# Routing to experts by pairs of positions: 128x128 transposes, a block-diagonal router, groups of 8 positions, ranks over 32, 24 and 7 positions

## What is computed

```
logits = xf @ Wr + br                       # 8064 rows x 64 experts
topk_logits, topk_idx = top_k(logits, 2)
gates = softmax(topk_logits)
for e in range(64):
    y = relu(xf @ W1[e] + b1[e]) @ W2[e] + b2[e]
    out = out + combine[:, e:e + 1] * y     # combine holds the gates of the two chosen
```

## Time and profile before

| | |
|---|---|
| median of 3 runs | 884.67 us (881.72 to 885.47) |
| the profiled execution: its own time | 888.75 us |
| the profiled execution: span, first to last instruction | 886.8 us |
| DVE busy | 645.4 us (73%) |
| POOL busy | 551.6 us (62%) |
| PE busy | 501.2 us (57%) |
| ACT busy | 339.2 us (38%) |
| granted clock of TensorE, mean | 0.741 |

### The profile page before, as it was taken

One profiled execution on the slowest core, in us unless ns is written; L12 is line 12 of the kernel. 1 busy time (PEld: TensorE's weight loads), 2 busy tenths in 40 slices (PEclk: granted clock), 3 DMA queues, 4 the chain that ended last, 5 costly groups with the idle time before them and its releaser, 6 DMA issues.

```text
span 886.8 us, 8725 instructions
## 1 busy us (share of the span) xinstructions
PE 501.2 (57%) x2132; PEld 320.0 (36%) x2132; DVE 645.4 (73%) x1160; ACT 339.2 (38%) x597; POOL 551.6 (62%) x398
## 2 busy tenths in 40 slices
PE   4916903365666665575556920002999999980340
PEld 3815801121211121121116910001777777760240
DVE  1379548999999989999974999991444444459951
ACT  2311384555555455454527710000444444430110
POOL 1002204699999999999940007777777167757774
PEclk9965655677787787878785555555999999995565
DMA  6999900000000000000000000302899899961131
GB/s 229 366 136 108 30 0 0 0 0 0 1 0 0 0 0 0 0 0 0 0 0 1 1 0 27 89 25 62 229 262 265 230 256 263 269 192 26 25 99 37
DMA packets 100734, 71.63 MB, mean 81 GB/s; under 512 B 29330, under 2 KB 87314, under 8 KB 100690
## 3 DMA queue, kind: packets, MB, share of 16 engines
q1 hardware_dynamic: 73154, 54.39, 28.0%
q0 software_dynamic: 8064, 8.27, 3.5%
q10 hardware_dynamic: 19472, 8.47, 3.3%
HBM read 48.12 MB, written 29.29 MB: 87 GB/s over the span
## 4 chain that ended last, share of the span: by engine, by line
POOL 35%; PE 22%; DVE 15%; issue 15%; SPq 4%; DMA 4%; ACT 3%; POOLq 1%; DVEq 0%; ACTq 0%
POOL hh_ring L419 13%; PE ps L611 8%; POOL w_ring L404 8%; POOL sorted_rows L438 7%; POOL xt L446 7%; PE ps L600 4%; DMA x_w<-packed 3%; PE ps L470 3%; SPq L328 2%; PE ps L538 2%; DVE mi L1072 1%; PE ps L521 1%; PE ps L593 1%; DVE hh_ring L1004 1%; DVE w_ring L1060 1%
## 5 line engine op out<-in xcount | busy, mean ns | idle before, releaser
L538 PE MATMUL ps<-hh_ring,ident 128*128 128x512 f32 x272 | 181.7, 807 | 153.1 <-POOL hh_ring L419 116.4
L438 POOL DMA_INDIRECT sorted_rows<-xp,slot_i x126 | 122.1, 969 | 115.0 <-DVE slot_i L1098 76.9
L404 POOL TENSOR_TENSOR w_ring<-xt,bc 128x1024 f32<-128x1024 f32 x64 | 153.8, 2405 | 37.3 <-DVE xt L973 37.3
L446 POOL DMA_INDIRECT xt<-expert_out,slot_i x126 | 120.7, 958 | 65.6 <-issue 37.8
L419 POOL TENSOR_TENSOR hh_ring<-hh_ring,bc 128x1024 f32<-128x1024 f32 x63 | 148.4, 2356 | 17.9 <-DVE hh_ring L1004 14.6
L538 PEld LDWEIGHTS ps<-hh_ring,ident 128*128 128x128 f32 x272 | 58.2, 234 | 275.8 <-POOL hh_ring L419 184.7
L1004 DVE TENSOR_TENSOR_SCAN hh_ring<-ps,w_ring 128x1024 f32<-128x1024 f32 x64 | 145.9, 2280 | 0.1
L611 PE MATMUL ps<-x_w 128*128 128x192 f32 x504 | 117.0, 355 | 0.0
L744 ACT ACTIVATE ps<-dt_t,a_exp 128x1024 f32<-128x1024 f32 x64 | 71.5, 1118 | 79.9 <-DVE w_ring L982 79.9
L748 ACT ACTIVATE ps<-dt_t,a_exp 128x1024 f32<-128x1024 f32 x64 | 71.5, 1118 | 65.1 <-DVE hh_ring L1004 65.1
L1172 DVE COPY x_w<-ps 128x128 f32<-128x128 f32 x126 | 36.8, 292 | 72.0 <-PE ps L611 69.0
(11 more groups left out here) (174 smaller groups left out, 707.9 us busy)
## 6 DMA issues: line engine op xcount, KB each, us to landing
x_w<-packed SPq DMA_DIRECT2D x252, 96.5 KB
sorted_rows<-pad_rows SPq DMA_DIRECT2D x2, 4096.0 KB, 18.0
x_w<-sorted_rows SPq DMA_DIRECT2D x32, 256.0 KB
expert_out<-x_w ACTq DMA_DIRECT2D x126, 64.0 KB
packed<-in_L_ffn_W SPq DMA_DIRECT2D x3, 2048.0 KB, 36.2
x_w<-in_x SPq DMA_DIRECT2D x7, 448.0 KB, 10.1
sorted_rows<-xp,slot_i POOLq DMA_INDIRECT x126, 2.1
xt<-expert_out,slot_i POOLq DMA_INDIRECT x126, 2.4
```

The costliest lines, as they stand in the source:

```text
L404: pool.tensor_tensor(w_ring[:, k % 4, :].rearrange("p (d s) -> p d s", s=S), up3[:, bass.ds(c * DC, DC), :], bc[:, k:k + 1, :].broadcast_t ...
L438: pool.indirect_dma_start(out=sorted_rows[k], out_offset=bass.IndirectOffsetOnAxis(ap=slot_i[:, k, l:l + 1], axis=0), in_=xp1[:, l, 0:C], ...
L446: pool.indirect_dma_start(out=y[:, l, :], out_offset=None, in_=expert_out[k], in_offset=bass.IndirectOffsetOnAxis(ap=slot_i[:, k, l:l + 1] ...
L538: ins = pe.matmul(ps[:, i, :], ident[:, :], hh_ring[:, buf, i * BANK:(i + 1) * BANK], start=(k < 0), stop=(k == N - 1), skip_group_check=True)
```

## The change

- Norms are written without gaps, 64 elements for each position (`xn`, over the memory of `xp1`), so that two positions are one block of 128 columns. PE transposes two positions at once, and multiplies by a `wr` of 128 rows and 128 columns, which holds `Wr` twice on its diagonal. Position 63, which doesn't exist, is set to zero.
- The bias of the router is no longer a row of `wr`. It is loaded into all partitions (`br_b`), and POOL adds it to the logits after ACT's copy, group by group; DVE's choices wait for POOL (`s_lgc`), and PE's reuse of a bank waits for ACT (`s_lgr`, new).
- Groups have 8 positions (8 groups, the last has 7). The statistics go by parts of 8, 16, 16 and 23 positions, and ACT's copy of the last sums goes by the same parts.
- The ranks go over runs of 32, 24 and 7 positions. `rank_of` now also makes the counts and bases of its run, and PE adds up the counts of the three runs in PSUM. `iota_p` and `zero_p` are made earlier, and both choices use them; the running sum of the first choice adds zeros where it took a maximum with its mask.
- The portions of `slot_i` are groups 0, 1 to 3 and 4 to 7 (`QCUTS`).

`span_of(g)` is the positions of a group; `part_of(g)` and `run_of(g)` are the part and the run that hold it.

```diff
-CUTS = (0, 1, 4, NG)
+QG = 8
+NQ = -(-L // QG)
+QCUTS = (0, 1, 4, NQ)
+PARTS = ((0, 8), (8, 24), (24, 40), (40, L))
+RUNS = ((0, 32), (32, 56), (56, L))
...
+
+
+def span_of(g):
+    return slice(QG * g, min(QG * (g + 1), L))
+
+
+def part_of(g):
+    return [QG * g < z for a, z in PARTS].index(True)
+
+
+def run_of(g):
+    return [QG * g < z for a, z in RUNS].index(True)
 
...
-            sp.dma_start(wr[0:C, 0:E], Wr).then_inc(s_moew, 16)
-            sp.dma_start(wr[C:C + 1, 0:E], br.rearrange("(a e) -> a e", a=1)).then_inc(s_moew, 16)
+            sp.wait_ge(s_zero, 6)
+            for t in range(2):
+                sp.dma_start(wr[t * C:(t + 1) * C, t * E:(t + 1) * E], Wr).then_inc(s_moew, 16)
+            sp.dma_start(br_b[:, :], br.rearrange("(a e) -> a e", a=1).broadcast_to([P, E])).then_inc(s_moew, 16)
...
+            pool.wait_ge(s_moew, 16 * 3)
+            for g in range(NQ):
+                v = logits[:, span_of(g), :]
+                pool.wait_ge(s_lgr, g + 1)
+                pool.tensor_tensor(v, v, br_b[:, :].unsqueeze(1).broadcast_to([P, v.shape[1], E]), ALU.add
+                                   ).then_inc(s_lgc, 1)
...
-                for j in range(GL):
-                    last = pe.matmul(t[:, j * P:(j + 1) * P], uT[:, g % GPC, j * P:(j + 1) * P], wr[:, :],
+                    pe.wait_ge(s_lgr, g - 1)
+                for j in range(QG // 2):
+                    last = pe.matmul(ps[:, 4 + g % 2, j * P:(j + 1) * P], nT[:, g % 3, j * P:(j + 1) * P], wr[:, :],
                                      start=True, stop=True)
                 last.then_inc(s_lg, 1)
...
-                for j in range(GL):
-                    last = pe.transpose(t[0:C + 1, j * P:(j + 1) * P], xp1[:, g * GL + j, 0:C + 1], ident[:, :])
+                for j in range(QG // 2):
+                    l = QG * g + 2 * j
+                    last = pe.transpose(ps[:, g % 2, j * P:(j + 1) * P], xn[:, l:l + 2, :].rearrange("p l d -> p (l d)"),
+                                        ident[:, :])
...
-                pe.wait_ge(s_cnt, k + 1)
-                pe.wait_ge(s_uTc, 2 * NG)
-                pe.matmul(ps[:, 0, 0:E], ones[:, :], small[:, 0, :], start=True, stop=True).then_inc(s_tot, 1)
-                pe.matmul(ps[:, 1, 0:E], tri[:, :], small[:, 0, :], start=True, stop=True).then_inc(s_tot, 1)
+                for c in range(len(RUNS)):
+                    first, last = c == 0, c == len(RUNS) - 1
+                    pe.wait_ge(s_cnt, len(RUNS) * k + c + 1)
+                    one = pe.matmul(ps[:, 0, 0:E], ones[:, :], seg[:, 0, c, :], start=first, stop=last)
+                    two = pe.matmul(ps[:, 1, 0:E], tri[:, :], seg[:, 0, c, :], start=first, stop=last)
+                    if last:
+                        one.then_inc(s_tot, 1)
+                        two.then_inc(s_tot, 1)
...
-            sum_out(NDC - 1)
+            act.wait_ge(s_add, NDC * (N + 1) + ADD_CR)
+            for a, z in PARTS:
+                act.activation(hg[:, a:z, (NDC - 1) * DC:C].rearrange("p l d -> p d l"),
+                               banks(0, 2).rearrange("p (d s) -> p d s", s=S)[:, :, 1 + a:1 + z], ACT.Copy
+                               ).then_inc(s_h2, 1)
...
+                act.wait_ge(s_nmr, part_of(g) + 1)
+                for l in range(QG * g, min(QG * (g + 1), L)):
...
 
                 act.wait_ge(s_uT, NG + g + 1)
...
+                if g >= 3:
+                    act.wait_ge(s_lg, g - 2)
+                act.activation(nT[:, g % 3, :], ps[:, g % 2, :], ACT.Copy).then_inc(s_uTc, 1)
...
+            for g in range(NQ):
+                if g + 1 < NQ:
+                    if part_of(g + 1) != part_of(g):
+                        std(part_of(g + 1))
                     norm(g + 1)
-                if g < NG:
-                    uT2_copy(g)
+                nT_copy(g)
                 if g > 0:
                     logits_copy(g - 1)
...
-            dve.wait_ge(s_h2, NDC + H2_CR)
             dve.wait_ge(s_consts, 3)
+            dve.memset(xn[:, L, :], 0.0).then_inc(s_zero, 1)
...
             def stats_of(c):
 
-                for l in range(CL * c, CL * (c + 1)):
+                a, z = PARTS[c]
+                dve.wait_ge(s_h2, NDC - 1 + c + 1 + H2_CR)
+                for l in range(a, z):
...
-            for c in range(CHUNKS):
-                if c + 1 < CHUNKS:
-                    stats_of(c + 1)
-                scales_of(c)
             dve.tensor_copy(iota_e[:, :], iota_e_i[:, :]).then_inc(s_dve, 1)
             dve.tensor_copy(tile_no[:, :], tile_no_i[:, :]).then_inc(s_dve, 1)
             ch.at = ch.at + 2
+            for c in range(len(PARTS)):
+                stats_of(c)
+                if c == 0:
+                    ch.link(dve.tensor_copy(iota_p, iota_e[:, :]))
+                    ch.link(dve.memset(zero_p, 0.0))
+                scales_of(c)
+
+            cnt, base = (seg[:, i] for i in range(2))
+            tot01, tiles, ends, before, zero, under = (small[:, i, :] for i in range(6))
...
-                ch.link(dve.tensor_copy(top[:, 2 + k, span], mi[:, span, k]))
-                m = mask[k][:, c]
-                flat = m.rearrange("p e l -> p (e l)")
-                iota, other = (iota_e[:, :], flat) if k == 0 else (iota_p, zero_p.broadcast_to([P, E * CL]))
-                ch.link(dve.tensor_tensor(m, iota.unsqueeze(2).broadcast_to([P, E, CL]),
-                                          top[:, 2 + k:3 + k, span].broadcast_to([P, E, CL]), ALU.is_equal))
-                ch.link(dve.tensor_tensor_scan(rank[k][:, c].rearrange("p e l -> p (e l)"), flat, other, 0.0,
-                                               ALU.add, ALU.max if k == 0 else ALU.add))
-
...
-                        dve.max_index(mi[:, l, :], mx[:, l, :], logits[:, l, :]).then_inc(s_dve, 1)
-                    ch.at = ch.at + GL
+                a, z = RUNS[c]
+                n = z - a
+                ch.link(dve.tensor_copy(top[:, 2 + k, a:z], mi[:, a:z, k]))
+                m, r = mask[k][c], rank[k][c]
+                ch.link(dve.tensor_tensor(m, iota_p.unsqueeze(2).broadcast_to([P, E, n]),
+                                          top[:, 2 + k:3 + k, a:z].broadcast_to([P, E, n]), ALU.is_equal))
+                ch.link(dve.tensor_tensor_scan(r.rearrange("p e l -> p (e l)"), m.rearrange("p e l -> p (e l)"),
+                                               zero_p.broadcast_to([P, E * n]), 0.0, ALU.add, ALU.add))
+                dve.tensor_copy(cnt[:, c, 0:1], r[:, 0:1, n - 1]).then_inc(s_dve, 1)
+                dve.tensor_tensor(cnt[:, c, 1:E], r[:, 1:E, n - 1], r[:, 0:E - 1, n - 1], ALU.subtract).then_inc(s_dve, 1)
+                ch.at = ch.at + 2
                 dve.wait_ge(s_dve, ch.at)
-                rank_of(0, c)
-
-            upto, cnt, base = (seg[:, i] for i in range(3))
-            tot, tot01, tiles, ends, before, zero, under = (small[:, i, :] for i in range(7))
-            ch.link(dve.memset(zero, 0.0))
-
-            iota_p, zero_p = ps[:, 6, 0:E], ps[:, 6, E:E + 1]
-            base_p = ps[:, 3, 0:CHUNKS * E].rearrange("p (c e) -> p c e", e=E)
+                dve.sem_inc(s_cnt, 1)
+                ch.link(dve.tensor_tensor(base[:, c], cnt[:, c], r[:, :, n - 1], ALU.subtract))
+                if c > 0:
+                    ch.link(dve.tensor_tensor(base[:, c], base[:, c], cnt[:, 0] if c == 1 else tot01, ALU.add))
+                if c == 1:
+                    ch.link(dve.tensor_tensor(tot01, cnt[:, 0], cnt[:, 1], ALU.add))
...
+            def choose(g):
+
+                v = span_of(g)
+                dve.wait_ge(s_lgc, g + 1)
+                for l in range(v.start, v.stop):
+                    dve.max(mx[:, l, :], logits[:, l, :]).then_inc(s_dve, 1)
...
-                ch.link(dve.tensor_tensor(tot01, cnt[:, 0], cnt[:, 1], ALU.add))
-                dve.tensor_tensor(tot, tot01, cnt[:, 2], ALU.add).then_inc(s_cnt, 1)
-                ch.link(dve.tensor_tensor(base, cnt, upto, ALU.subtract))
...
-                for g in range(NG):
-                    c, a = g // GPC, GL * (g % GPC)
-                    m = mask[k][:, c, :, a:a + GL]
-                    span = slice(GL * g, GL * (g + 1))
-                    r = ps[:, 4 + g % 2, 0:E * GL].rearrange("p (e l) -> p e l", l=GL)
...
-            for c in range(CHUNKS):
...
+            for g in range(NQ):
+                choose(g)
+                if span_of(g).stop == RUNS[run_of(g)][1]:
+                    rank_of(0, run_of(g))
             place(0)
             dve.tensor_tensor(top[:, 0, :], mx[:, :, 1], mx[:, :, 0], ALU.subtract).then_inc(s_ediff, 1)
```

More of the change, by code:

```diff
@@ new lines, in choose @@
+            def choose(g):
[3 more added lines that the diff above has]
+                    dve.max(mx[:, l, :], logits[:, l, :]).then_inc(s_dve, 1)
+                ch.at = ch.at + v.stop - v.start
+                dve.wait_ge(s_dve, ch.at)
+                for l in range(v.start, v.stop):
```

(3 more changed lines are left out.)

114 lines of the change are left out of this document (47 added, 67 removed).

## The result

The changed kernel takes 889.42 us (median of 20 runs, 882.54 to 893.80), the kernel before 886.24 beside it (20 runs): ratio 1.0039, 95% interval 1.0022 to 1.0056. That is 3.5 us slower, 1.9 to 5.0 (the two medians lie 3.2 apart). The forecast was 885.8, 1.1 above the 884.67 of before, in a range that ended at 889.5. The time is inside the range by 0.1 us, but the forecast's "no change that can be told" did not hold: the interval lies above 1. Of the 3.6 us between 885.8 and 889.42, 1.6 is the kernel before itself, whose median is 886.24 here and was 884.67. The profiled execution took 890.42 us with a span of 888.2, against 888.75 and 886.8.

A forecast was written before the change was run, and what follows sets the result against it. The prediction took the first dispatch on POOL, waiting for `slot_i` through ACT's and DVE's work, to move the end one for one. Terms -1.4 + 1.5 + 0.5 + 0.5 = +1.1 on 884.67 gave 885.8 us, range 881 to 889.5.

The forecast's parts named there:

- DVE from the first choice to the first dispatch: DVE's work from first MAX8 to POOL's first dispatch: choices -0.2, ranks 0, counts +0.4, first `place` group +0.3; sum +0.5.
- the cast: Head of the first `rank_of`: the cast meets POOL's sixth add, costing 0 to 1.2 us, taken as +0.5.
- the counts: Counting work moved from `place` into each run's `rank_of`: 2.95 us before, 3.34 after, taken as +0.4.
- the start of the choices: First MAX8 on DVE: -1.4 from ACT's order, +1.5 from operations blocked by adds, so 485.3 instead of 485.21.
- the group of `place`: First group of `place` on DVE has 8 positions: 2.49 us becomes 2.77, +0.3.
- the locks: DVE's second scale operation, parts 2 and 3, blocked by a POOL add: about 0.75 us later each, +1.5 together.
- The rival of blocked choices: POOL's adds also block MAX8 and FIND_INDEX8: 5 x 1.2 on top of +1.1, 891.8 us; chance 0.10.
- nothing is blocked: Rival: POOL's adds miss DVE's small operations by chance of time; -0.9, 883.8 us; chance 0.22.
- The choices and ranks: DVE's choices in nine groups took 21.84 us, now eight take 21.6 (-0.2); ranks stay at 14.37; the cast adds 0.5.
- The rival that reads 32 apart cost more: Reduce over experts in `place`: the price grows with read distance, 1.2 us more per first-run group; 888.8 us, chance 0.08.
- After the dispatch: POOL's 63 dispatches run without a gap; the next 24 slots are ready 1.8 us before they are wanted.
- The rival of unblocked choices: DVE's choices no longer wait for the last root: first dispatch 4.1 us earlier, 880.6 us; chance 0.05.

The follow-up runs named there:

- a3: Changed kernel without the router's bias and POOL's eight adds; ratio to the kernel before 0.9980, last copy of sums to first dispatch 70.36 us.
- a4: Changed kernel with ACT's roots for parts 2 and 3 ahead of the logit copy they stood behind; ratio to the kernel before 0.9966.
- a2: Changed kernel with the wait closing each group of choices kept only ahead of a rank; ratio to the kernel before 0.9990.
- a5: Changed kernel with early roots for parts 2 and 3, the last two groups ahead, and part 3's statistics before part 2's scales; ratio to the kernel before 0.9948.
- c2_before: Kernel before, unchanged, timed against itself on a chip where it takes 885.87 us; 887.14 us, ratio 1.0013.
- h1: Kernel before with one more, unused load (the router's bias) on SP's queue at its head, behind a wait; ratio to the kernel before 1.0020.
- a7: Changed kernel with two runs, 32 and 31 positions; one run, 1071.74 us on a chip where the kernel before takes 1082 to 1083.
- a8: Changed kernel with runs of 24, 24 and 15 positions; one run, 1078.90 us on a chip where the kernel before takes 1082 to 1083.
- a1_again: Changed kernel, unchanged, on another chip where the kernel before takes 1082 to 1083 us; ratio to the kernel before 1.0009.
- c1_after: Changed kernel, unchanged, once more on a chip where the kernel before takes 885.87 us; 888.46 us, ratio to the kernel before 1.0021.

## Why the prediction was right or wrong, point by point

**The total.** Four comparisons of the change give +3.5, +1.0, +1.6 and +1.9 us. Only the first has an interval that leaves out zero. Weighted by their intervals they make 2.2 with an uncertainty of 0.9 (an estimate that takes them as independent), so the change is slower, by 1.3 to 3.2; before against itself gave -1.4 and +1.2. The forecast's +1.1 was 0.2 under what the stretch shows and some 1 us under this mean. What the forecast took for too small to tell, 0.5% (4.4 us), was set too wide: 20 runs of each kernel tell 0.39% from nothing.

**The step that failed** is "DVE from the first choice to the first dispatch": with the cast +1.0 forecast (+0.5 and +0.5), +1.72 measured (47.27 for 45.55). It gave the choices -0.2, and they took +0.4; it gave the counts +0.4, and they took +0.9. The mechanisms of the sum held, the sizes of these two terms did not. That the sum still came within 0.2 us of the stretch is luck: the start of the choices missed by 0.5 the other way, and the group of `place` by 0.3. The second step is that the prediction put everything outside the routing at nothing; what the first comparison shows beyond the stretch, 2.2 us, no run assigns.

**Start of the choices: +0.1 forecast, -0.44 measured.** The mechanism held: norms 5 us earlier counted from the copy (4.02 against 9.51), first MAX8 nearly where it was, the rest given back at the root of the last part. The size was off by 0.5: norms start 0.3 earlier than forecast, the locks cost 1.37 (0.92 and 0.81 less twice 0.18) instead of 1.5, and ACT's seven copies took 3.3 instead of 3.4.

**The locks: right, and the cause is shown** by a3 (gone without adds) and a4 (gone when the root moves). The Trainium skill (SBUF — State Buffer, section "Who interferes with whom") says that a DVE operation with two SBUF inputs, or a copy or cast in a two-port mode, contends with GpSimd, and one with at most one SBUF input outside these modes doesn't. The runs agree: 0.92, 0.81 and the cast's 0.61 to 1.01 beside an add of 1.26, MAX8 at 1.11 to 1.12 with or without one. In which mode the cast runs, no trace shows. The rival of blocked choices (+6.0 more) fell with it, and "nothing is blocked" as well.

**The choices and ranks: +0.3 forecast, +0.82 measured** (485.69 to 525.03 less the counts of two runs, 37.15, against 36.33 from 485.21 to 521.54). The cast gave its share, +0.4. The choices took 22.35 against 21.94, +0.4, where the forecast has 21.6 against 21.84 (it took all three rounds at 7.28; the second was 7.39). The error is in "7 groups of 8 at 8/7 of 2.43 (2.74)": 2.43 is a third of a chunk, which ended with one wait, and now every group ends with one. That is eight waits instead of three, five more at 0.11 each (a2), 0.55. The kernel's text shows it: in the new `choose` the last wait stands at the end of each group.

**The counts: +0.4 forecast, +0.91 measured** (0.79 + 1.40 + 1.67 = 3.86, for 2.95). The terms were 0.64, 1.16 and 1.53: each run's small operations took 0.14 to 0.24 more, for the most part DVE's wait for its own strided subtract (0.15 behind line 1108). **The group of `place`: +0.3 forecast, +0.01 measured** (2.50), since the reduce took 1.01 for 512 elements, less than 1.13 for 448. These two misses, 0.5 and 0.3, cancel in part.

**The rival that reads 32 apart cost more: wrong**, in sign too for 32; see the last section. **After the dispatch: right**, no gap after the eighth, 81.37 to the read back.

**The rival of unblocked choices (880.6): the order on DVE and ACT spoke against it, rightly**; a5 shows that the time lay there, 4.6 us against the kernel before (66.31 for 70.87), where 4.1 were priced.

**Outside the routing.** The forecast put nothing there. The two first traces differ by 0.92 at the copy of sums, but the traces of both programs spread over 65.5 to 68.8 in the projections, and c2_before has the long value: this part isn't shown to belong to the change. The copy of sums starts at 460.81 and 460.25 in the two traces of the changed kernel where before takes 885 us, and at 459.89 and 460.28 in those of before. On the other two chips it starts at 455.2 to 458.8 in nine traces of the changed kernel and its variants (mean 457.1) and at 454.5 to 456.2 in three of before or h1 (mean 455.5). That hints at a loss ahead of the copy, but one trace differs from the next by as much. Why the clock rises in some executions and not in others wasn't tried. Whether the mean of 2.2 holds a further us beside the stretch's 1.28 stays open.

## What to carry to other kernels

When an operation moves to another engine, look for what starts on the other engines while it runs: beside an add of 1.26 us on POOL a 0.18 us operation of DVE became one of 0.9, and because its start was released by the same engine as the add, it happened each time. Before a stage is made finer, find which item of the other engine's written order is really waited for: an order that serves the last part's root early was worth 5.8 us, while the finer tiling with the order as it stood moved the start of the choices by 0.4. And count fixed costs per piece, waits on oneself included: a third run cost 2 us, a wait 0.11 a group.

## What the hardware did that was not expected

**The reduce over a strided read.** The sum over 64 experts costs, per group of eight positions: 1.01 when the neighbours lie 32 elements apart, 1.06 at 31, 1.43 at 24, 1.29 at 21 (1.13 for seven positions, in proportion), 1.09 at 7 (0.95 for seven), 1.01 at 15. The price does not rise with distance. The reduces grouped by shape (count, busy time, mean ns), first where the runs are 32 and 31 (a7), then where they are 24, 24 and 15 (a8):

```profile
L1171 DVE TENSOR_REDUCE top<-hh_ring 128x8 f32<-128x512 f32 x7 | 7.2, 1027 | 0.2
```

and

```profile
L1171 DVE TENSOR_REDUCE top<-hh_ring 128x8 f32<-128x512 f32 x7 | 9.6, 1369 | 0.2
```

The first seven are four of 1.00 and three of 1.06, the second six of 1.43 and one of 1.01 (15 apart).

The Trainium skill (SBUF — State Buffer, "Door 1: The DMA port swizzle") says that each access which crosses to a new line of 16 bytes pays a penalty. All these distances cross one with every element, and no single penalty fits both 1.01 and 1.43; the measurement decides. Its cause wasn't tried.

**The same program on other chips.** On two chips the experts took 353 us (read back to second gather) instead of 185, for both kernels. The windows row from 614 to 700 us, in which POOL dispatches the second choice, on such a chip (a1_again) and on the other (c1_after):

```profile
614.00:700.00 86.00, 12.25 (x44) 8.43 (x44) 8.39 (x23) 2.80 (x9) 58.91 (x61) 0.52 0.12 39
```

and

```profile
614.00:700.00 86.00, 83.17 (x502) 62.34 (x502) 35.23 (x110) 36.37 (x113) 59.90 (x62) 0.90 0.84 235
```

POOL's dispatches are as busy in both, 58.91 and 59.90, but PE runs 44 matmuls instead of 502 and the DMA share is 0.12 instead of 0.84. The waits of PE there, up to 12.9 us each, have no releaser that the trace shows. From 700 on, with POOL idle, a1_again's PE is busy 73.87 of 80 us. What holds the other engines back during the dispatches on one chip and not on another wasn't tried; a ratio is safe only against runs of the same chip.
